# Softmax sums on four column strips of TensorE, with a copy step before the reciprocal

## What is computed

```python
q = jnp.einsum('bnd,hde->bhne', query, Wq) * scale
k = jnp.einsum('bmd,hde->bhme', query, Wk)
v = jnp.einsum('bmd,hde->bhme', query, Wv)
logits = jnp.einsum('bhne,bhme->bhnm', q, k)
attn = jax.nn.softmax(logits, axis=-1)
out = jnp.einsum('bhnm,bhme->bnhe', attn, v)
```

## Time and profile before

| | |
|---|---|
| median of the runs | 1905.37 us |
| the profiled execution | 1907.01 us, its span 1905.2 us |
| TensorE matmul busy | 1841.5 us (97%) |
| VectorE busy | 1223.7 us (64%) |
| ScalarE busy | 859.1 us (45%) |
| GpSimd busy | 1344.2 us (71%) |
| mean granted TensorE clock | 0.988 |

### The profile page before, as it was taken

The page is one execution under the profiler, slowest core; times in us unless marked ns, Lnnn a source line. Parts: engine busy times, 40 slices in busy tenths (PEclk is TensorE's granted clock), DMA queues, the critical chain, the costliest instruction groups (busy, mean ns, idle before and its releaser), DMA issues.

```text
span 1905.2 us, 30739 instructions
## 1 busy us (share of the span) xinstructions
PE 1841.5 (97%) x11400; PEld 1175.7 (62%) x11400; DVE 1223.7 (64%) x2147; ACT 859.1 (45%) x1101; POOL 1344.2 (71%) x719
## 2 busy tenths in 40 slices
PE   7899999999999999999999999999999998999998
PEld 5555555555665565556666565556665554598887
DVE  5466655666766657756666657666666667765565
ACT  3344444444435443344345533343444543465674
POOL 1688787778666867697678767797668676662564
PEclk9899999999999999999999999999999999999999
DMA  4210000002312000022211000021111011444340
GB/s 139 85 40 18 23 18 23 18 23 74 99 29 62 23 18 23 23 64 88 78 44 41 18 23 7 32 81 56 45 44 37 17 34 34 153 125 134 128 133 34
DMA packets 132142, 104.24 MB, mean 55 GB/s; under 512 B 58140, under 2 KB 118684, under 8 KB 130972
## 3 DMA queue, kind: packets, MB, share of 16 engines
q1 hardware_dynamic: 128924, 93.81, 16.6%
q0 software_dynamic: 3072, 8.46, 1.2%
HBM read 69.15 MB, written 29.43 MB: 52 GB/s over the span
## 4 chain that ended last, share of the span: by engine, by line
PE 83%; DVE 5%; POOL 5%; issue 3%; ACT 2%; DMA 1%; SPq 0%; POOLq 0%; DVEq 0%; ACTq 0%
PE score_ps L1127 23%; PE av_ps L1141 21%; PE spare_ps L1090 9%; PE spare_ps L1106 8%; PE spare_ps L1083 5%; PE spare_ps L441 4%; PE y_ps L1704 3%; PE h_ps L1675 3%; PE spare_ps L1152 3%; POOL prob_sum L1011 3%; DVE max_of L1283 1%; PE spare_ps L490 1%; PE spare_ps L465 1%; POOL expert_rows L430 1%; POOL wp_lo L1437 1%
## 5 line engine op out<-in xcount | busy, mean ns | idle before, releaser
L1011 POOL TENSOR_TENSOR prob_sum<-prob_sum,probs 128x1024 f32<-128x1024 f32 (+1 forms) x384 | 905.8, 2359 | 202.6 <-ACT probs L1227 170.6
L1283 DVE TENSOR_REDUCE max_of<-spare_ps 128x1 f32<-128x512 f32 x1024 | 656.6, 682 | 346.5 <-PE spare_ps L1106 335.6
L1227 ACT ACTIVATE probs<-score_ps 128x1024 f32<-128x1024 f32 x512 | 502.8, 1025 | 686.6 <-PE score_ps L1127 671.5
L1141 PE MATMUL av_ps<-probs,v 128*64 128x512 f32 x2048 | 488.0, 602 | 3.0 <-ACT probs L1227 1.6
L1141 PEld LDWEIGHTS av_ps<-probs,v 128*64 128x64 f32 x2048 | 129.8, 136 | 241.6 <-issue 221.1
L1007 POOL TENSOR_TENSOR prob_sum<-probs 128x1024 f32<-128x1024 f32 (+1 forms) x64 | 150.2, 2347 | 146.9 <-ACT probs L1227 146.8
L1106 PE MATMUL spare_ps<-k_hi,q_hi 64*128 64x512 f32 x1024 | 230.6, 443 | 21.9 <-DVE max_of L1283 21.1
L1106 PEld LDWEIGHTS spare_ps<-k_hi,q_hi 64*128 64x128 f32 x1024 | 99.6, 185 | 224.6 <-issue 189.2
L1127 PE MATMUL score_ps<-q_hi,k_hi 64*128 64x512 f32 x1024 | 211.7, 407 | 1.1 <-DVE o_in L1333 0.9
L1127 PE MATMUL score_ps<-shift_rows,ones 64*128 64x512 f32 x1024 | 205.7, 395 | 0.0
L1127 PE MATMUL score_ps<-q_lo,k_hi 64*128 64x512 f32 x1024 | 205.4, 394 | 0.0
(11 more groups left out here) (249 smaller groups left out, 2367.7 us busy)
## 6 DMA issues: line engine op xcount, KB each, us to landing
o_transposed<-o_out SPq DMA_DIRECT2D x64, 256.0 KB, 2.0
v<-in_L_ffn_W_dram SPq DMA_DIRECT2D x16, 1024.0 KB, 6.0
o_in<-o_transposed SPq DMA_DIRECT2D x28, 512.0 KB, 4.1
w_raw<-in_L_attn_Wq_dram SPq DMA_DIRECT2D x64, 64.0 KB, 2.3
w_raw<-in_L_attn_Wk_dram SPq DMA_DIRECT2D x64, 64.0 KB, 2.2
wv_raw<-in_L_attn_Wv_dram SPq DMA_DIRECT2D x32, 128.0 KB, 2.8
shift_rows<-neg_rows SPq DMA_DIRECT2D x256, 1.0 KB
x<-in_x_dram SPq DMA_DIRECT2D x4, 1024.0 KB, 5.9
```

The costliest lines, as they stand in the source:

```text
L1011: pool.tensor_tensor(out, out, probs[:, n % RING, heads], ALU.add).then_inc(prob_added, 1)
L1141: last = pe.matmul(av_ps[hd * E:(hd + 1) * E, :], v[:, quad % 2, kt, 2 * first_head + hd, :], probs[:, n % RING, hd, :], start=(kt == 0), ...
L1227: act.activation(probs[:, n % RING], score_ps[n % 2][:, :, :], ACT.Exp).then_inc(probs_ready, 1)
L1283: dve.tensor_reduce(max_of[:, u % 2, kh, j, hd:hd + 1], bank[:, :], AX.X, ALU.max).then_inc(pass_read, 1)
```

## The change

A sum is now four matmuls instead of two; they have 32 result columns each and 256 query columns: head and half of the queries choose one of four strips of 32 partitions of the bank, and half the bank's columns are used. The turn covers 256 columns. Each strip of denominators is then copied to both strips of its head, by a `tensor_reduce` over one element, which makes eight such instructions per unit; they run on 32 partitions with 8 elements each. One reciprocal over all 128 partitions follows, in place, and the spreading as before. In the step lists the inversion of the sums of line 2 moves from line 2 to line 3, behind its first pass, and the normalisation of line 3 moves from before the two scores to behind the second pass.

```diff
@@ -655,8 +655,8 @@
 STEPS = tuple(tuple(line.split()) for line in (
     "early av av av pass score score pass sum av recip pass score score pass late bite bite",
     "bite norm score pass early av pass score score pass score pass late av av av",
-    "av pass score score pass early av sum pass score score pass bite late av recip av",
-    "pass norm score score pass early bite bite av pass score score pass late av av av"))
+    "av pass score score pass early av sum pass score score pass bite late av av",
+    "pass recip score score pass norm early bite bite av pass score score pass late av av av"))
@@ -686,11 +686,17 @@
     BLOCK = 32
+    HALF = BANK // 2
+    HEAD_HALVES = ((0, 0), (0, 1), (1, 0), (1, 1))
@@
+    def strip(hd, half):
+
+        return slice((2 * hd + half) * BLOCK, (2 * hd + half + 1) * BLOCK)
@@ -1148,9 +1155,9 @@
                 take(("sum", u), [(sum_turned, u + 1)])
-                for hd in range(2):
-                    last = pe.matmul(bank[hd * E:(hd + 1) * E, :], ones[:, 0:E], prob_sum[:, u % 2, hd, :],
-                                     start=True, stop=True)
+                for hd, half in HEAD_HALVES:
+                    last = pe.matmul(bank[strip(hd, half), 0:HALF], ones[:, 0:BLOCK],
+                                     prob_sum[:, u % 2, hd, half * HALF:(half + 1) * HALF], start=True, stop=True)
                 last.then_inc(sum_ready, 1)
@@ -1309,11 +1316,18 @@
-                dve.transpose(sums[:, :], bank[:, :]).then_inc(sum_turned, 1)
+                dve.transpose(sums[:, 0:HALF], bank[:, 0:HALF]).then_inc(sum_turned, 1)
 
             def invert(u):
                 dve.wait_ge(sum_turned, u + 1)
-                dve.reciprocal(inverse[:, :], sums[:, 0:BANK:BLOCK]).then_inc(recip_done, 1)
+                blocks = HALF // BLOCK
+                for hd, half in HEAD_HALVES:
+                    for other in range(2):
+                        dve.tensor_reduce(inverse[strip(hd, other), half * blocks:(half + 1) * blocks],
+                                          sums[strip(hd, half), 0:HALF:BLOCK].rearrange("p (c a) -> p c a", a=1),
+                                          AX.X, ALU.add).then_inc(sum_copied, 1)
+                dve.wait_ge(sum_copied, 2 * len(HEAD_HALVES) * (u + 1))
+                dve.reciprocal(inverse[:, :], inverse[:, :]).then_inc(recip_done, 1)
                 dve.wait_ge(recip_done, u + 1)
```

More of the change, by code:

```diff
@@ L854, in build_attention @@
         sum_turned = sem("sum_turned")
+        sum_copied = sem("sum_copied")
         recip_done = sem("recip_done")
```

## The result

The changed kernel takes 1979.21 us (median of four runs, 1977.23 to 1982.05), against 1905.64 us for the kernel before in the same session: the ratio is 1.0373, with a 95% interval from 1.0359 to 1.0388. I had forecast 1939 us with a range up to 1956. The sign was right, and the size less than half of what came. The profiled execution has a span of 1978.5 us, 73.3 more than before, and a mean granted clock of 0.983 instead of 0.988.

A forecast was written before the change was run, and what follows sets the result against it. TensorE's instruction stream bounds the attention part. Odd units 27.9, even units 4.0, late places 2.6 and -1.9, and the end 0.7 sum to 33.3 us on 1905.4: 1939 us, range 1896 to 1956.

The forecast's parts named there:

- The sum on TensorE: Four strips side by side save 0.43 us per unit, less 0.15 for one more change of tile shape: 0.28.
- Rival (b): The strips don't run four at a time: 13 us more in the even units, 1952 us; chance 0.09.
- The copies: Eight new reductions per unit on VectorE, not overlapping, at 0.17 us each: 1.36 us, 1.39 with the wait.
- Rival (a): The copies overlap at 0.066 us from start to start: 7 us faster, 1898 us; chance 0.18.
- the odd term: Loss of the 31 odd units, each 8c - 0.47 us with c for one copy: 27.9 us in all.
- Odd units: The half's last pass on TensorE waits for a bank read behind the copies, 0.9 us late in 31 units: 27.9 us.
- rival (c): A later TensorE wait in the odd half shrinks by as much as the pass is late: about 1911 us; chance 0.07.
- Even units: First product with v waits for the late normalisation, up to 0.56 us: 12.4 of stalls less 8.4 saved, net +4.0.
- Special places: Three even units where VectorE was already late, +2.6 in one and -1.9 in two; the last unit's end +0.7 us.

The follow-up runs named there:

- no_copies: The changed kernel without its eight copies, the reciprocal reading each partition's own strip (exchange between strips left out): 1887.5 us, ratio 0.9897 to the kernel before.
- one_strip: The changed kernel with its copies replaced by eight same-size reductions, all from strip 0 to strip 0 of scratch (exchange left out): 1919.87 us, ratio 1.0068.
- even_early: The changed kernel with the even units' inversion back in line 2, behind the first pass after the sum, normalisation in its old place: 1941.17 us, ratio 1.0167.
- both_moved: The changed kernel with the even units' inversion as in even_early and the odd units' inversion behind the last pass: 1910.35 us, ratio 1.0008.

## Why the prediction was right in sign and wrong in size

**The sum on TensorE: right.** 0.28 forecast, 0.27 measured, from the timeline and from no_copies. From the sum to the product 0.34 is saved (0.91 to 0.57), and from the product to the pass 0.07 is lost (0.96 to 1.03). The four strips do run together: the first records of the four begin within 0.02 us. Rival (b) falls.

**The copies: right mechanism, a little too cheap.** 0.17 forecast, 0.19 measured; 1.52 us with the wait instead of 1.39. Rival (a), overlapping copies, falls by one_strip against the change. At 0.19 the odd term is 31 x 1.05.

**Odd units: right place, too small.** I forecast this pass 0.9 us late, and it is 1.02. But I priced only its beginning. The projection step behind a pass that had to wait begins 0.22 us later after it than in an unbroken stream, so an odd unit loses 1.24 us: some 38 us in 31 units, and not 27.9. That nothing makes it up (rival (c)) held: even_early kept this loss, and both_moved took it away.

**Even units: the step that failed.** The prediction says "What is late is av_ps". I looked at one thing that waits behind the moved inversion, the normalisation, and that one is about as late as I said. But the inversion was put in front of a read, and each read frees a bank that some later step takes. I did not ask which. It is the second projection step of the same half, which comes 1.9 us after the second pass (275.18 to 277.04), while the first product comes 3.3 after it. Worked out from the rows of before, the read would have begun at 274.81 + 1.39 + 0.29 + 0.64 = 277.13 and the step at 277.9; against 277.04 that is 0.9 us late, in nearly every even unit, and not 0.56 in 19 of them. The trace has 1.02 up to the product, and less the shorter sum an even unit loses 0.76 us (2.00 for the pair, less 1.24), where I had 4.0 / 30 = 0.13. Over 30 units this is 23 us instead of 4, and these 19 us are the largest part of the error of 40. A misreading of mine matters little beside it: of the even units, 3 have the 5.79 us from pass to product and 6 the longer stretch, not 6 and 5, which makes my stalls 11.5 us instead of 12.4.

**Special places: the terms right, the same step missed once more.** Timeline of PE in the changed kernel, unit 28, then unit 60:

```profile
806.92 0.50 PE L1113 MATMUL spare_ps<-k_hi,q_hi 64*128 64x512 f32 x2 [1.27 <-DVE max_of L1290]
...
810.47 0.70 PE L1097 MATMUL spare_ps<-xT_kept,w_hi 128*128 128x512 f32 x2 [1.33 <-issue]
...
1662.81 0.49 PE L1113 MATMUL spare_ps<-k_hi,q_hi 64*128 64x512 f32 x2 [1.28 <-DVE max_of L1290]
1667.55 1.97 PE L1148 MATMUL av_ps<-probs,v 128*64 128x512 f32 x4 [4.25 <-DVE o_out L1340]
```

The wait before the late pass fell from 2.19 and 2.16 us to 1.27 and 1.28, the 0.9 that I forecast. In unit 60 the wait on o_out grew from 0.66 to 4.25; the two together are +2.7, where I had +2.6. In unit 28 a wait of 1.33 us on the bank is new, the step that I had missed.

**The granted clock: not priced.** From 100 us to the end of the attention the kernel before has three stretches of 3.4 us at clock 0.50, at 778, 1191 and 1604 us; there matmuls of the scores start 0.43 us apart instead of 0.23, so a stretch costs up to 1.6 us. Each of the three comes within 3 us behind a pass that had waited 2.2 us. Timeline of PE before, behind the wait of unit 60:

```profile
1604.86 0.63 PE L1127 MATMUL score_ps<-q_hi,k_hi 64*128 64x512 f32 x2
1605.29 0.63 PE L1127 MATMUL score_ps<-q_lo,k_hi 64*128 64x512 f32 x2
```

The changed kernel has six of them, at 698, 722, 777, 1128, 1152 and 1207, and two of 6.8 us at 1664 and 1688. The one at 698 comes right behind this (timeline of PE, changed kernel):

```profile
694.93 0.66 PE L479 MATMUL spare_ps<-ident,x 128*128 128x128 f32 x4
697.41 0.48 PE L1090 MATMUL spare_ps<-wv_hi,xT_kept 128*128 128x256 f32 x2 [1.83 <-issue]
```

An extra step of the batch before takes a bank there, so the first projection step already meets the late one, and TensorE stands still for 1.83 us. The 24 us more at half clock cost at most 24 x (1 - 0.23 / 0.43) = 11 us; this is an estimate from the rows, and no run took the clock apart from the waits.

**The sum again.** The 31 pairs grew by 67.2 us: 31 x 2.00 = 62, 10.7 more in the four pairs with the stretches at 698 to 777 and 1128 to 1207 (they grow by 5.5, 3.9, 5.4 and 3.9), and 5.5 less in the others together, such as that of unit 28, where the stretch at 778 is gone. From the last pair on it is 7.8 us more, with the stretch at 1688, and 1.7 less ahead of the first product: 73.3, the difference of the spans.

## What to carry to other kernels

When work on an engine moves ahead of a read, list every buffer that this read and the ones behind it free, find who takes each next, and price the one that has the least slack, not the most obvious one. Count copies between partitions by their length on an engine whose reads gate a busy TensorE: here each us past the slack cost 2 us per pair, and halving the count and moving the inversion behind the reads turned a loss of 3.7% into a gain of 0.8%. A wait can cost more than its gap: here the next step also started later, and behind some waits, of 1.15 to 2.2 us, the granted clock was 0.50 for 3.4 us.

## What the runs showed of the hardware

- Reductions of 32 partitions by 8 elements start 0.074 us apart when all read one strip of 32 partitions and all write one, even if the two differ, and 0.187 apart when the strip read or the strip written changes, in the order of the program (1.47 us for eight instead of 0.67).
- Four fp32 matmuls with 32 result columns and 256 moving columns on four column strips take 0.57 us to the next product, where two with 64 and 512 took 0.91.
- Behind the last pass of the odd units, which had to wait, the next step begins 0.55 us after the pass where it is a projection to q or k (18 units) and 0.50 where it is a step of the other layers (12 units). In the kernel before, in an unbroken stream, it was 0.33 in both, but for one unit (0.55). In the last unit, with scores behind the pass, it was 0.31 with the wait and 0.35 without, so this holds for these steps alone.
